# Output experts with one masked tile per expert, and norms, key gate and feature shift on ScalarE

## The reference

```python
x = layernorm(x + mamba_block(x))                  # strand A; two norms inside it
gates = sigmoid(x @ w_gate)                        # 8 heads x 8 experts, per token
gm = one_hot(argmax(gates)) * gates                # one expert per token and head
values = einsum('bhne,ehdk,bnd->bhnk', gm, value_experts, x)
attn = softmax(causal(q @ k.T / 8))
out = einsum('bhij,bhjk->bhik', attn, values)
out = einsum('bhne,ehkd,bhnk->bhnd', gm, output_experts, out).sum(heads)
x = layernorm(x + out)                             # strand B; norm lnB
q, k = gelu(x @ Wq.T + bq) + 0.21, gelu(x @ Wk.T + bk) + 0.21
x = layernorm(x + linear_attention(q, k, v))       # strand C; norms lnC, lnD
x = layernorm(x + soft_experts(x))                 # second block, over all sequences
```

## Time and profile before

| what | value |
|---|---|
| median of 3 runs | 1579.16 us (1578.62 to 1583.59) |
| profiled execution | 1580.04 us, its span 1578.1 us |
| TensorE busy | 1438.5 us, 91% of the span |
| VectorE busy | 1214.6 us, 77% |
| ScalarE busy | 820.8 us, 52% |
| GpSimd busy | 790.4 us, 50% |
| L636, b_out on TensorE | 2048 records, 275.8 us busy |
| L1360, b_mo on VectorE | 248 instructions, 166.3 us busy |

### The profile page before, as it was taken

One profiled execution on the slowest core, in us unless ns is written; L12 is line 12 of the kernel. 1 busy time (PEld: TensorE's weight loads), 2 busy tenths in 40 slices (PEclk: granted clock), 3 DMA queues, 4 the chain that ended last, 5 costly groups with the idle time before them and its releaser, 6 DMA issues. The chain is left out here.

```text
span 1578.1 us, 32322 instructions
## 1 busy us (share of the span) xinstructions
PE 1438.5 (91%) x10752; PEld 1261.2 (80%) x10752; DVE 1214.6 (77%) x2335; ACT 820.8 (52%) x1846; POOL 790.4 (50%) x1959
## 2 busy tenths in 40 slices
PE   5588999999999999999999999946999999869997
PEld 4366788788788788788788787836999999869997
DVE  4466798898898898898898887764888888736664
ACT  2234544544544544544544544303777776557774
POOL 0332253553553553553553552222777777557763
PEclk9998999999999999999999999966999999989999
DMA  6000000000000000000000000008676667877782
GB/s 236 7 7 1 8 1 14 15 1 14 15 1 15 15 1 14 15 1 15 15 1 15 8 1 8 8 7 252 171 197 188 185 186 199 254 266 301 300 316 71
DMA packets 140752, 132.10 MB, mean 84 GB/s; under 512 B 7376, under 2 KB 130512, under 8 KB 134096
## 3 DMA queue, kind: packets, MB, share of 16 engines
q1 hardware_dynamic: 140624, 130.50, 26.1%
HBM read 73.85 MB, written 56.62 MB: 83 GB/s over the span
## 5 line engine op out<-in xcount | busy, mean ns | idle before, releaser
L636 PE MATMUL bk<-ve_f,oe 128*128 128x128 f32 x2048 | 275.8, 279 | 0.8 <-DVE ve_f L1360 0.8
L636 PEld LDWEIGHTS bk<-ve_f,oe 128*128 128x128 f32 x2048 | 248.9, 192 | 23.4 <-issue 20.1
L2287 POOL TENSOR_TENSOR d_s<-d_ex 128x1024 f32<-128x1024 f32 x32 | 131.8, 4120 | 100.8 <-ACT d_ex L2087 100.8
L1360 DVE SCALAR_TENSOR_TENSOR ve_f<-ps_m,oT 128x512 f32<-128x512 f32 x248 | 166.3, 678 | 3.7 <-PE bk L636 2.3
L1321 DVE COPY_PREDICATED vals<-oh,bk 128x1024 f32<-128x1024 int32 x112 | 146.6, 1309 | 10.3 <-PE bk L404 8.5
L2037 PE MATMUL d_sl<-d_ex,e_prT 128*128 128x128 f32 x1024 | 136.0, 277 | 8.8 <-POOL d_ex L2304 8.8
L1971 PE MATMUL d_lg<-d_phf,d_xtf 128*128 (+1 forms) x1024 | 128.1, 287 | 14.4 <-DVE d_ex L2191 7.6
L1971 PEld LDWEIGHTS d_lg<-d_phf,d_xtf 128*128 128x128 f32 x1024 | 125.1, 203 | 15.2 <-issue 11.1
L2037 PEld LDWEIGHTS d_sl<-d_ex,e_prT 128*128 128x128 f32 x1024 | 125.4, 193 | 9.0 <-POOL d_ex L2304 9.0
L1981 PE MATMUL d_sl<-d_ex,d_xs 128*128 128x128 f32 x1024 | 121.3, 277 | 5.8 <-DVE d_ex L2202 5.8
L1981 PEld LDWEIGHTS d_sl<-d_ex,d_xs 128*128 128x128 f32 x1024 | 118.4, 194 | 6.2 <-DVE d_ex L2202 6.2
(11 more groups left out here) (340 smaller groups left out, 3730.5 us busy)
## 6 DMA issues: line engine op xcount, KB each, us to landing
logits<-d_raw SPq DMA_DIRECT2D x128, 256.0 KB, 3.3
e_lt<-logits SPq DMA_DIRECT2D x32, 1024.0 KB, 5.1
y_slots<-d_ys SPq DMA_DIRECT2D x64, 256.0 KB, 4.3
d_ex<-y_slots SPq DMA_DIRECT2D x16, 1024.0 KB, 6.8
d_w<-W SPq DMA_DIRECT2D x16, 256.0 KB, 3.4
oe<-xT SPq DMA_DIRECT2D x1, 2048.0 KB, 7.9
xt_in<-xT SPq DMA_DIRECT2D x16, 128.0 KB, 2.3
x_in<-x SPq DMA_DIRECT2D x16, 128.0 KB, 2.4
```

Source lines behind the costliest of these rows:

```text
L636: last = pe.matmul(ps_u[:, cols], oe[:, hp, e, :], mo[:, n % MO, hp, :], start=False, stop=(e == NE - 1 and hp == HP - 1), skip_group_chec ...
L1360: V.scalar_tensor_tensor(mo[:, n % MO, :, :].rearrange("p a n -> p (a n)"), chosen_of(b, c), float(NE - e), oT[:, u, c, :, :].rearrange("p ...
L2287: G.tensor_tensor(s8[:], part[:, 0:8, :], part[:, 8:16, :], ALU.add).then_inc(n, 1)
```

## The change

The output experts are done for both chunks of a batch at once. `b_choice` is called for both chunks in the first half of TensorE's slot, and a new function `b_m` on ScalarE copies each into a bfloat16 tile `chosen` in SBUF. `b_mo` then makes one tile of 128x1024 for each expert, with chunk as the inner dimension, and `b_out` multiplies 256 columns in two halves of two head pairs. MO is 3 (tiles twice as wide).

`scale_rows` moves to ScalarE for ln1, lnB and lnC, as an Identity activation with pointer scale rstd and pointer bias -mean*rstd. VectorE writes that bias (`shift`) and waits for the rows in `a_ln1` and `c_ln`. ScalarE does `a_na` behind b_probs(3), `c_ncn` behind b_probs(5) and `b_x2` behind a_st.

The key gate isn't multiplied into `vals` on GpSimd (`b_vg` is gone) but into the transposed probabilities, as the pointer scale of `b_pt`, which is now two activations for each head (256 and 128 columns). The feature shift `c_q` moves from VectorE to ScalarE, between c_gelu and a_cin. `sz` and `tz` share a tile, as do `ya` and `yg`; `pr` has one of its own; the tiles of the preparation lie inside `lx` and `mx`.

```diff
-MO = 4
-OUTS = C * NE
+MO = 3
...
-        pr = ve_f[:, 2048:3584].rearrange("p (q s a n) -> p q s a n", q=2, s=2, a=3)
+        pr = sb("pr", [2, 2, 3, P])
...
-        oT = sb("oT", [2, C, HP, P])
+        oT = sb("oT", [2, HP, C, P])
+        chosen = sb("chosen", [HP, C, P], BF16)
...
-        def scale_rows(dve, n, src, dst, b):
-            wait(dve, norms[n]["rstd"], RSQRT_OPS * (b + 1))
+        def shift(dve, n, b):
+            dve.wait_ge(norms[n]["rstd"], RSQRT_OPS * (b + 1))
+            dve.scalar_tensor_tensor(nb[n][:], nbuf[n][1][:, :, 0], -1.0, rstd_of(n)[:], ALU.mult, ALU.mult
+                                     ).then_inc(norms[n]["shift"], 1)
+
+        def scale_rows(act, n, src, dst, b):
+            act.wait_ge(norms[n]["shift"], b + 1)
             for c in range(C):
-                dve.tensor_scalar(dst[:, c, :], src[:, c, :], nbuf[n][1][:, c, 0:1], rstd_of(n)[:, c:c + 1],
-                                  ALU.subtract, ALU.mult).then_inc(norms[n]["rows"], 1)
+                nc.scalar.activation(dst[:, c, :], src[:, c, :], ACT.Identity, scale=rstd_of(n)[:, c:c + 1],
+                                     bias=nb[n][:, c:c + 1]).then_inc(norms[n]["rows"], 1)
...
 # TensorE
-                    pe.wait_ge(q["b_vg"], C * (b + 1))
+                    pe.wait_ge(q["b_v"], (NE - 1) * (b + 1))
...
+            def b_out(b, e, half):
+                n = NE * b + e
+                if half == 0:
+                    pe.wait_ge(q["b_mo"], n + 1)
+                for hp in (2 * half, 2 * half + 1):
+                    last = pe.matmul(ps_u, oe[:, hp, e, :], mo[:, n % MO, hp, :], start=False,
                                      stop=(e == NE - 1 and hp == HP - 1), skip_group_check=True)
...
                 if c:
                     b_oat(t - 3)
+                if o:
+                    b_choice(t - 2, u, 1)
...
 # ScalarE
-                copy(pt[:, s, a, :, :].rearrange("p a b -> p (a b)"), ps_v[0][:, a, 0:3 * P]
-                     ).then_inc(q["b_pt"], 1)
+                nc.scalar.activation(pt[:, s, a, 0:2, :].rearrange("p a b -> p (a b)"), ps_v[0][:, a, 0:2 * P], ACT.Copy,
+                                     scale=gx[:, 0, h:h + 1])
+                nc.scalar.activation(pt[:, s, a, 2, :], ps_v[0][:, a, 2 * P:3 * P], ACT.Copy, scale=gx[:, 1, h:h + 1]
+                                     ).then_inc(q["b_pt"], 1)
...
+            def b_m(b, c):
+                act.wait_ge(q["b_m_ps"], C * b + c + 1)
+                wait(act, q["b_mo"], NE * b)
+                copy(chosen[:, :, c, :], ps_m[:].rearrange("p (a n) -> p a n", a=HP)).then_inc(q["b_m"], 1)
...
+            def c_q(b):
+                act.wait_ge(q["c_g"], 2 * (b + 1))
+                wait(act, q["c_out_ps"], b)
+                nc.scalar.activation(ql[:], gl[:], ACT.Copy, bias=SHIFT).then_inc(q["c_q"], 1)
...
                 if a:
                     a_lx(t, 0)
+                if o:
+                    b_m(t - 2, 0)
...
                     a_lx(t, 1)
+                if o:
+                    b_m(t - 2, 1)
...
                     b_probs(t - 1, 3)
+                if a:
+                    a_na(t)
...
                     b_probs(t - 1, 5)
+                if c:
+                    c_ncn(t - 3)
+                if b:
                     b_rgs(t - 1, 1)
...
 # VectorE
+            def b_mo(b, u, e):
+                n = NE * b + e
                 if e == 0:
-                    dve.wait_ge(q["b_m_ps"], C * b + c + 1)
-                if n == 0:
+                    dve.wait_ge(q["b_m"], C * (b + 1))
                     dve.wait_ge(q["b_ot"], HP * (b + 1))
-                wait(dve, q["b_oe"], OUTS * b + n - MO + 1)
+                wait(dve, q["b_oe"], n - MO + 1)
+                V.scalar_tensor_tensor(mo[:, n % MO, :, :].rearrange("p a n -> p (a n)"),
+                                       chosen[:].rearrange("p a c n -> p (a c n)"), float(NE - e),
+                                       oT[:, u, :, :, :].rearrange("p a c n -> p (a c n)"), ALU.is_equal, ALU.mult
                                        ).then_inc(q["b_mo"], 1)
...
                 if o:
-                    b_mo(t - 2, u, 0, 6)
+                    b_mo(t - 2, u, 3)
                 if b:
                     b_max(t - 1, 1)
-                if o:
-                    b_mo(t - 2, u, 0, 7)
+                if a:
+                    shift(dve, "ln1", t)
                 if a:
                     a_ln1(t)
                 if o:
-                    b_mo(t - 2, u, 1, 0)
+                    b_mo(t - 2, u, 4)
                 if more:
                     a_sz(t + 1)
                 if b:
                     b_ot(t - 1, 1 - u, 0)
-                if o:
-                    b_mo(t - 2, u, 1, 1)
+                if c:
+                    shift(dve, "lnC", t - 3)
                 if b:
                     b_max(t - 1, 2)
                     b_rg(t - 1, 1)
                 if c:
                     c_ln(t - 3)
                 if o:
-                    b_mo(t - 2, u, 1, 2)
+                    b_mo(t - 2, u, 5)
...
                     b_ot(t - 1, 1 - u, 1)
                 if o:
-                    b_mo(t - 2, u, 1, 3)
-                    b_mo(t - 2, u, 1, 4)
+                    b_mo(t - 2, u, 6)
                 if b:
                     b_max(t - 1, 3)
```

More of the change, by code:

```diff
@@ L290, in token_blocks @@
         q = {n: sem(n) for n in names}
-        norms = {n: {k: sem(f"{n}_{k}") for k in ("moments", "rstd", "rows")}
-                 for n in ("rms", "ln1", "ln2", "lnB", "lnC", "lnD")}
+        norms = {n: {k: sem(f"{n}_{k}") for k in ks.split()}
+                 for n, ks in (("rms", "rstd"), ("ln1", "moments rstd shift rows"), ("ln2", "moments rstd"),
+                               ("lnB", "moments rstd shift rows"), ("lnC", "moments rstd shift rows"),
+                               ("lnD", "moments rstd"))}
+        nb = {n: sb(f"{n}_b", [C]) for n in ("ln1", "lnB", "lnC")}
         nbuf = {n: (sb(f"{n}_st", [C, 6]), sb(f"{n}_mv", [C, 2]), sb(f"{n}_v", [C]), sb(f"{n}_h", [C]),
@@ L612, in b_choice @@
                     pe.wait_ge(q["b_oht"], b + 1)
[L613 to L616, removed]
+                wait(pe, q["b_m"], C * b + c)
                 rows = slice(64 * c, 64 * c + 64)
                 for hp in range(HP):
-                    last = pe.matmul(chosen_of(b, c)[:, hp * P:(hp + 1) * P], pick[rows, hp, :, :].rearrange("p a k -> p (a k)"),
+                    last = pe.matmul(ps_m[:, hp * P:(hp + 1) * P], pick[rows, hp, :, :].rearrange("p a k -> p (a k)"),
                                      ohT[rows, u, :], start=True, stop=True, skip_group_check=True)
@@ L628, in b_start @@
                           skip_group_check=True).then_inc(q["b_start"], 1)
-            def b_out(b, c, e):
-                n = NE * c + e
-                cols = slice(c * P, (c + 1) * P)
-                pe.wait_ge(q["b_mo"], OUTS * b + n + 1)
-                for hp in range(HP):
-                    last = pe.matmul(ps_u[:, cols], oe[:, hp, e, :], mo[:, n % MO, hp, :], start=False,
+            def b_out(b, e, half):
[4 more added lines that the diff above has]
+                    last = pe.matmul(ps_u, oe[:, hp, e, :], mo[:, n % MO, hp, :], start=False,
                                      stop=(e == NE - 1 and hp == HP - 1), skip_group_check=True)
-                last.then_inc(q["b_oe"], 1)
+                if half == 1:
+                    last.then_inc(q["b_oe"], 1)
             def b_oat(b):
@@ L1109, in slot @@
                     c_gelu(t - 3)
+                    c_q(t - 3)
                 if more:
@@ L1173, in _ @@
             slot(NB // 2, 0, False, True, True, True, False)
+            b_m(Z, 0)
+            b_m(Z, 1)
+            b_x2(Y, 0)
             b_x2t(Y, 0)
             c_gelu(Y)
+            c_q(Y)
             b_oa(Z)
             c_kr(Y)
+            b_x2(Z, 1)
             b_x2t(Z, 1)
             c_gelu(Z)
+            c_q(Z)
+            c_ncn(Y)
             c_kr(Z)
             c_x3t(Y)
+            c_ncn(Z)
             c_x3t(Z)
@@ L1508, in slot @@
                 if o:
-                    b_mo(t - 2, u, 0, 0)
+                    b_mo(t - 2, u, 0)
                 if a:
@@ L1517, in slot @@
                 if c:
-                    b_x2(t - 3, 1 - u)
+                    shift(dve, "lnB", t - 3)
                 if b:
@@ L1608, in slot @@
                 if o:
-                    b_mo(t - 2, u, 1, 6)
+                    b_mo(t - 2, u, 7)
                 if b:
@@ L1659, in _ @@
             c_res(Y, 0)
-            b_x2(Z, 1)
-            c_q(Z)
+            shift(dve, "lnB", Z)
+            shift(dve, "lnC", Y)
             c_v(Z)
@@ L1668, in _ @@
             rsqrt(dve, "lnC", Z, 1.0, 1e-12, norms["lnC"]["moments"], 2 * C)
+            shift(dve, "lnC", Z)
             c_ln(Z)
```

164 lines of the change are left out of this document (62 added, 102 removed).

## The result

| what | before | after |
|---|---|---|
| median of four runs | 1579.66 us (1578.62 to 1583.59) | 1666.26 us (1660.88 to 1666.88) |
| ratio to before | | 1.054, interval 1.051 to 1.056 |
| profiled execution, span | 1580.04, 1578.1 us | 1660.88, 1658.6 us |
| VectorE busy | 1214.6 us, 77% | 1189.2 us, 72% |
| ScalarE busy | 820.8 us, 52% | 914.3 us, 55% |

The change costs 86.6 us between the medians, where 72.8 were forecast. The time lies in the slots: 69.8 of the 80.5 us of span between the start of slot 3 and that of slot 15, 2.9 before them, 7.8 behind.

The account below looks back on a forecast made before the run. The slot was taken as a loop of TensorE, 18.2 us of VectorE in order, ScalarE, then TensorE. 1580.0 plus 52.4 (4.37 in twelve slots), 10 for the other slots and 10 for the clock gave 1652 us, range 1614 to 1680.

Parts of the forecast that it names:

- front, up to a_res: TensorE's first half of the slot: b_choice(1) moved in adds 0.33 us, c_q on ScalarE 0.10, lnB's norm nothing.
- b_mo in front of b_max(1): VectorE: a whole wide tile stands where one half tile of 0.60 us stood, +0.55 a slot.
- hand-over of ln1: After b_max(1), VectorE waits for ScalarE's norm queued behind two probabilities: +1.61 us a slot.
- hand-over of lnC: VectorE waits for ScalarE's lnC norm behind probabilities 4 and 5: +1.65 us a slot.
- to b_max(3), the wait of a_ln2 in it: VectorE, b_max(2) to b_max(3): two whole tiles replace three halves, +0.50 us; the wait before a_ln2 is swallowed, -0.27.
- tail: TensorE behind the wait at b_rgb: four groups of wider output matmuls on the path save 0.20 us a slot.
- clock, in twelve slots: TensorE's longer idle holes halve its clock in half of twelve slots, 1.7 us each: 10 us, ends 0 and 20.
- Rival (a): The wide masked tile runs at double rate, taking 0.6 us: 2.2 us a slot, 1616 us; chance 0.12.
- rival (b): Faster, since TensorE sets the slot and the wait at b_rgb disappears: about -1.5 us a slot, 1559 us; chance 0.07.
- (c): The clock falls twice a slot, holding TensorE's first half too: 41 us in place of 10, 1683 us; chance 0.11.
- (d): Nothing to see: copies and waits balance, the hand-overs lying in slack, 1580 us; chance 0.03.
- The signs named ahead: VectorE idle 2 to 2.5 and near 2 us before two norm products; b_rgb wait 2 to 3; slot 63 to 65.

Follow-up runs that it names:

- b1: The kernel before with only the norms of ln1 and lnC moved to ScalarE, at the places the kernel after gives them; 1631.2 us, 1.033 of before.
- e2: The kernel after with the same instructions, only VectorE's order changed so that independent work stands ahead of the products of ln1 and lnC; 1634.7 us, 1.033 of before.
- p1: The kernel after with the masked tile comparing the choice in PSUM, the second chunk's for both chunks; 1666.3 us, 1.054 of before.
- e3: The kernel after with the feature shift back on VectorE, ahead of the seventh choice of values; 1672.1 us, one run.
- t1: The kernel after with all three norms and the feature shift back on VectorE, the gate staying in the probabilities' copies; 1640.2 us, 1.037 of before.
- e1: The kernel after with the norms of ln1 and lnC computed on VectorE again; 1638.5 us, 1.037 of before.

## Why the prediction was right, and where it was off

The direction, the cause named first and the range held. The size was 73 against 87 us. By the steps of the sum, each measured as the median over the twelve full slots of the time from the slot's start, stretched slots left out at the end (the rows above, less the slot start 585.73, agree within 0.03):

| step | predicted | measured |
|---|---|---|
| front, up to a_res (choice 0.33, c_q 0.10, lnB 0) | 0.43 | 1.25 |
| b_mo in front of b_max(1) | 0.55 | 0.55 |
| hand-over of ln1 | 1.61 | 1.68 |
| from there to b_max(2) | 0.10 | -0.05 |
| hand-over of lnC | 1.65 | 1.71 |
| to b_max(3), the wait of a_ln2 in it | 0.23 | 0.47 |
| tail | -0.20 | -0.10 |
| slot | 4.37 | 5.51 |
| clock, in twelve slots | 10 | 4.3 |

- **The hand-overs** were read right, place and price, and b1 shows them by themselves: 3.43 measured, 3.26 summed. The price of the norm on ScalarE was a little low (0.81 against 0.89 for two). The 0.46 for one was also not what its working gives: 0.564 less 128 columns at the rate between the two rows is 0.37, and 0.46 is about the middle of them. e2 shows that their cause is VectorE's order and not ScalarE's work.
- **The wide tile.** Its duration (1.21 against 1.23 forecast) and its shifts (0.55, and 0.47 for 0.50) came. Rival (a) is refuted: the tile with the bf16 operand takes 1.21, L1213 with two float32 operands 1.23, and the tile with an operand in PSUM 1.21. By the rule that the prediction quoted from the Trainium skill (Vector Engine (DVE) Microarchitecture Reference, Points that are easy to get wrong) the first would have been the fast one; the measurement decides against it.
- **The front is the mis-sized step.** The prediction saw that the new tile holds GpSimd up "by about a microsecond" eight times. It then asked only whether the root of ln1 was waited for, and put up to 0.3 a slot in the range. But the RMS root releases the residual, and lnB's root stands in front of the product mx, which in turn holds the shift of lnB. That shift had been costed at 0.15 with other work beside it. The hold was put at nothing in the sum for the front, and removing it alone takes 0.76 off the front (p1); of what is left, 0.49, some 0.4 stands there already at the first choice of values (596.53, 10.80 into the slot, against 10.41 before), behind the b_choice that had been priced at 0.33. Giving c_q back gained nothing, since the RMS root then releases the residual (e3). In the kernel as changed the hold costs 0.78 a slot, 9 us in twelve slots, which in p1 the clock took back; without the norms it costs 1.69. The Trainium skill (SBUF — State Buffer, Who interferes with whom) also says which side waits: issue order decides who blocks. The trace agrees in both directions: GpSimd's step of 1.15 us started 0.13 after the tile that held it, and VectorE's shift of 1.22 started 0.08 after GpSimd's product. The prediction used the rule in one direction only.
- **The costs don't add.** Norms alone 3.43, the rest with the tile 3.31 (t1), together 5.51: 1.23 less than the sum, because while VectorE waits for ScalarE, GpSimd's late roots are made up for. lnB's norm and the feature shift are in neither part, but they cost nothing here: e1 has them on ScalarE and t1 doesn't, 62.36 and 62.35. e1 showed the other face: removing the hand-overs returned 2.19 and not 3.39.
- **The wait of 0.27 in front of a_ln2** was taken off as if every slot had it. It belonged to the one longer slot that was read; without it the step would have said 0.50, against 0.47 measured. The wait of 1.21 at b_rgb was that slot's too; the usual 0.82 makes rival (b)'s gain 0.4 a slot smaller.
- **The clock** was priced a little high per stretch (1.42 in after, 1.7 taken) and too often: three slots in the profiled execution, six forecast. p1, b1, e1 and t1 had nine, three, five and six, so a number near six wasn't unreasonable, but these rows don't show what decides it within one kernel: the same wait of 2.48 us was followed by a fall in one slot of after and not in the one before it. Whether a different count makes the 5 us between the profiled execution and the median was not tried.
- **A part of the hit is luck.** Twelve slots cost 13.7 us more than forecast and the clock 5.7 less; with 0.7 more in the small slots and 0.6 off for two longer slots of the kernel before, the profiled execution is 8.1 above its forecast. Had six slots been stretched, as forecast, it would have been some 12.
- **The other rivals** fell too: VectorE's order and not TensorE sets the slot (b), the clock fell at most once in a slot (c), and the hand-overs were in no slack (d). The signs named ahead came: waits of 2.2 and 2.25, 2.48 at b_rgb, slots of 64.55.
- Slots 0 to 2, 15, 16 and everything behind: 10 predicted, 2.9 and 7.8 measured in the span.

## What to carry to other kernels

When an operand moves from PSUM to SBUF and an instruction of VectorE then reads two SBUF operands, look up what GpSimd does in that time, and who waits for it: here 1.2 us products held 0.2 us steps of the roots for which the residual and two more norms wait. Of work that is handed to another engine, ask what stands ahead of it in that engine's queue; the same instructions in an order that puts independent work behind the hand-over gave back 32 of 87 us. And don't add up what two changes cost alone: together they cost 1.2 us a slot less than that.

## What the runs showed of the hardware

- A VectorE SCALAR_TENSOR_TENSOR of 1024 columns takes 1210 ns with bf16 and f32 in SBUF, 1210 with f32 in PSUM and in SBUF, and 1226 with two f32 in SBUF (L1213).
- GpSimd steps of 0.20 us last to the end of a VectorE product with both operands in SBUF (up to 1.32), whether one operand is bf16 or both are f32 (0.69 beside L1395), and not beside one with an operand in PSUM (no step of lnB's root over 0.35 in the slot of p1 from 591.25). The other way round, two VectorE instructions were held by GpSimd: the shift of lnB (1.22), and in t1 a wide tile that took 1.76 beside GpSimd's xb product:

```profile
525.29 1.76 DVE L1388 SCALAR_TENSOR_TENSOR ve_f<-chosen,oT 128x1024 f32<-128x1024 bf16 x1
```

```profile
525.04 0.92 POOL L1704 TENSOR_TENSOR xb<-x_in,lnb 128x256 f32<-128x256 f32 x1
```

- A ScalarE norm of 128 columns with both pointer operands takes 0.46 (lnB) to 0.51 us (ln1), and two in a row 0.89.
- A stretch of TensorE at 1.2 GHz lasted 3.4 us and cost 1.4 to 1.8 us of the slot. In full slots it came only in the kernels in which TensorE had stood idle for 1.75 to 2.5 us at b_rgb just before, and not behind each such wait (3 of 12 in after, 9 of 12 in p1).
